# Order of h_lo, conv taps and scan input products in the first half of each tile of a gated-SSM and ternary-FFN kernel

## The reference

```
# block 1
z  = layernorm(x);  u, v = split(z @ in_proj_w + in_proj_b)          # 512 -> 2 x 512
v  = silu(v);       vl = depthwise_conv3(v) + conv_b                   # along time
h_t = a * h_{t-1} + ssm_b * vl_t;   y_t = ssm_c * h_t + ssm_d * vl_t    # scan along time
g  = (u * silu(y)) @ out_proj_w + out_proj_b
x  = x + layernorm(layernorm(g + z) * ln_w + ln_b)
# block 2, weights W1 and W2 rounded to -1, 0, 1 by their mean absolute value
h  = gelu(layernorm(x) @ W1.T + b1)                                    # 512 -> 2048
x  = x + layernorm(h @ W2.T + b2)                                      # 2048 -> 512
```

## Time and profile before

| | us |
|---|---|
| median of 3 runs | 1448.06 (1447.77 to 1449.75) |
| the profiled execution, its own time | 1449.17 |
| its span, first to last instruction | 1447.1 |
| TensorE busy | 1406.8 (97%) |
| VectorE busy | 1118.3 (77%) |
| ScalarE busy | 875.6 (61%) |
| GpSimd busy | 449.6 (31%) |

### The profile page before, as it was taken

The page is one execution under the profiler, slowest core; times in us unless marked ns, Lnnn a source line. Parts: engine busy times, 40 slices in busy tenths (PEclk is TensorE's granted clock), DMA queues, the critical chain, the costliest instruction groups (busy, mean ns, idle before and its releaser), DMA issues. The chain is left out here.

```text
span 1447.1 us, 18964 instructions
## 1 busy us (share of the span) xinstructions
PE 1406.8 (97%) x6492; PEld 635.1 (44%) x6492; DVE 1118.3 (77%) x1891; ACT 875.6 (61%) x1261; POOL 449.6 (31%) x522
## 2 busy tenths in 40 slices
PE   6998999999999999999999999999999999999997
PEld 4443444444444444444444444444444444443443
DVE  8898886877968677786877968678786877998634
ACT  7887665655656566565655656566565655753443
POOL 5146132331523315132321523215142331522211
PEclk9999999999999999999999999999999999999999
DMA  9612221221113112121131113112121221001200
GB/s 264 206 55 80 48 77 29 49 69 30 59 30 88 30 30 80 18 78 30 46 72 29 59 30 88 29 30 80 22 74 30 44 73 30 29 1 30 58 30 30
DMA packets 155984, 82.00 MB, mean 57 GB/s; under 512 B 132720, under 2 KB 132720, under 8 KB 155760
## 3 DMA queue, kind: packets, MB, share of 16 engines
q1 hardware_dynamic: 155888, 80.79, 22.4%
HBM read 31.49 MB, written 16.78 MB: 33 GB/s over the span
## 5 line engine op out<-in xcount | busy, mean ns | idle before, releaser
L562 PE MATMUL f2b<-w,ring 128*128 128x512 fp8e5 x1008 | 382.7, 380 | 2.8 <-DVE w L1004 1.2
L563 PE MATMUL f2b<-w,ring 128*128 128x512 fp8e5 x1008 | 382.3, 379 | 0.0
L534 PE MATMUL f1b<-x3T,w 128*128 128x512 f16 x960 | 365.0, 380 | 6.6 <-DVE w L1004 3.0
L535 PE MATMUL f1b<-x3T,w 128*128 128x512 f16 x960 | 365.0, 380 | 0.0
L1283 ACT ACTIVATE ring<-f1b,par 128x512 f32<-128x512 f32 x256 | 175.0, 683 | 227.3 <-PE f1b L535 226.9
L1623 POOL TENSOR_SCALAR ve<-mv 128x4 f32<-128x4 f32 (+2 forms) x89 | 33.8, 380 | 716.1 <-DVE mv L706 715.8
L714 DVE SCALAR_TENSOR_TENSOR ring<-ring,f_sc 128x512 f16<-128x512 f32 x256 | 209.4, 831 | 41.2 <-ACT ring L1293 41.1
L1293 ACT ACTIVATE ring<-ring,f_sc 128x512 f16<-128x512 f32 x256 | 180.3, 711 | 0.0
L501 PE MATMUL misc<-x1T,win_hi 128*128 128x512 f16 x464 | 176.0, 379 | 2.2 <-DVE yb L807 1.4
L502 PE MATMUL misc<-x1T,win_hi 128*128 128x512 f16 x464 | 176.0, 379 | 0.0
L503 PE MATMUL misc<-x1T,win_lo 128*128 128x512 f16 x464 | 176.0, 379 | 0.0
(11 more groups left out here) (211 smaller groups left out, 2032.2 us busy)
## 6 DMA issues: line engine op xcount, KB each, us to landing
out_dram<-hb SPq DMA_DIRECT2D x64, 256.0 KB, 2.0
xs<-x_dram SPq DMA_DIRECT2D x14, 1024.0 KB, 5.4
ring<-w1t_dram SPq DMA_DIRECT2D x3, 1024.0 KB, 8.0
stage<-w2t_dram SPq DMA_DIRECT2D x3, 1024.0 KB, 8.1
x1T<-tp SPq DMA_TRANSPOSE x68, 3.1
xs<-x_dram SPq DMA_DIRECT2D x4, 256.0 KB, 3.3
stage<-w_in_dram SPq DMA_DIRECT2D x4, 256.0 KB, 5.0
xs<-x_dram SPq DMA_DIRECT2D x2, 512.0 KB, 6.6
```

What stands on the lines that cost most here:

```text
L534: pe.matmul(b[:, :], w, src[:, k, :], start=k == 0, stop=False)
L535: mm = pe.matmul(b[:, :], w, src[:, KC + k, :], start=False, stop=k == KC - 1)
L562: pe.matmul(f2b[q][:, :], h_hi[:, i % H_SLOTS, qs], w2[:, j, :], start=j == 0, stop=False)
L563: mm = pe.matmul(f2b[q][:, :], h_lo[:, i % H_SLOTS, qs], w2[:, j, :], start=False, stop=j == FC - 1)
```

## The change

Three numbers change. In the first half of every stage in which tile c is convolved (stages 2 to 15), VectorE issues lo(3) in front of tap 2 of channel block 2 instead of behind it. ScalarE issues d_conv(c, 2) behind gelu(6) and hi(5), and d_conv(c, 3) behind gelu(7) and hi(6); before, both stood in front of gelu(6). In stage 2 the Sign with the number 5.3 then stands in front of both, and the Sign with 6.5 between them. No instruction, wait or buffer changes.

```diff
-AT_LO = (1.2, 2.2, 2.32, 2.42, 3.36)
-AT_D_CONV, AT_CENTRE = (3.15, 3.16, 5.25, 5.3), (13.3, 13.5, 14.3, 14.5)
+AT_LO = (1.2, 2.2, 2.32, 2.38, 3.36)
+AT_D_CONV, AT_CENTRE = (3.15, 3.16, 6.15, 7.15), (13.3, 13.5, 14.3, 14.5)
```

## The result

Before 1448.13 us, after 1446.12 us (medians of 19 runs each); the ratio of all runs is 0.9983, 95% interval 0.9976 to 0.9989, or -2.5 us (-3.5 to -1.6); the medians alone are 2.0 us apart. The profiled execution took 1446.71 us, its span is 1444.7. The same kernel was measured once more beside the last experiments: 0.9986 (0.9977 to 0.9994), -2.0 us. So the change is a small gain, and it is the difference of two larger numbers.

The account below looks back on a forecast made before the run. TensorE, busy for 97% of the span, was taken to bound the kernel, so only its waits count. Steady stages -5.4 us plus stage 2 +2.6 us gave -2.8 us, 1445.3 us against the median of 1448.06; range 1442.6 to 1449.5 us.

Parts of the forecast that it names:

- The steady term: TensorE's waits at f2(3) and f1(8), mainly in stages 4 to 15, vanish: -5.4 us.
- The margin at f2(4): Steady stages: lo(4) ends 0.6 us before f2(4) wants it, so no new wait there.
- rival C: Steady stages: lo(4) comes late at f2(4), +0.5 us in ten stages, 1455.7 us; chance 0.08.
- Stage 2's rigid shift: Stage 2: later products delay the scans, piece 11 and f1(8), with nothing hiding it: +3.6 us.
- The clock's part: Stage 2: slow stretch falls on f2(3), f1(8) may run at full clock, so the stage costs +2.6 instead of +3.6.
- rival A: Stage 2: slow stretch stays in front of f1(8), full +3.6 us, sum -1.8, 1446.3 us; chance 0.25.
- The sum: Whole kernel: -5.4 us steady plus 2.6 us in stage 2 gives -2.8 us, 1445.3 us; chance 0.50.
- Two bounds of the prediction: Steady stages: lo(4) 1.0 us late gives 4.3 of 5.4 us back; range top 1449.5 us, gain half given back.
- B: Stage 2 costs nothing, as TensorE does not wait for the ternary pieces: -5.4, 1442.7 us; chance 0.08.
- D: Products land between the same neighbours, or gaps come from issuing; only stage 2 tells: 1448 to 1451.7 us; chance 0.09.

Follow-up runs that it names:

- dconv_only: Kernel before with only the ScalarE move: d_conv(2) behind hi(5), d_conv(3) behind hi(6), lo(3) unmoved; 1.0006, +0.9 us against before.
- lo4_late: stage2_old with lo(4) behind scan(2) instead of in front of it, in all stages; 1.0011, +1.6 us against before.
- stage2_only: Kernel before with the new d_conv order on ScalarE in stage 2 alone, lo(3) unmoved; 1.0027, +3.9 us against before.
- stage2_old: Changed kernel with the old d_conv order kept in stage 2, lo(3) swapped there too; 0.9957, -6.2 us, again 0.9964, -5.2 us against before.
- lo_only: Kernel before with only the VectorE swap: lo(3) in front of tap 2 of block 2; 1.0006 against before.
- lo56_early: stage2_old with ternary pieces 11 to 19, lo(5) and lo(6) in front of the scans in stage 2; 0.9953, -6.8 us against before.

## Why the prediction was right

**The steady term: right, slightly small.** Forecast -5.4 us; from stage 3 to the end the two profiles differ by 5.8 us. The transposes' waits at the starts of stages 8 and 14 are different in each execution, here 0.20 and 0.45 us instead of 0.44 and 0.22, by chance the same sum. The missing 0.4 us have two sources: the 20 distances, each less 0.216 us, sum to 5.15 us and not to 5.05, and some 0.02 us per stage lie in the distances right behind the two waits (0.22 to 0.23 us), which were not summed. A stage became 0.54 us shorter, not 0.50. dconv_only, which leaves the first wait, has half of the gain. The margin at f2(4) of 0.6 us, on which rival C hung, is confirmed by lo4_late. C did not come about: GpSimd's additions start 11.9 us into stage 7 and last 6.8 us in both kernels.

**Stage 2's rigid shift: right.** Forecast 3.6 us for piece 11, measured 3.64; less the 0.36 us by which stage 2 begins later, both products start at the forecast times (111.05 and 114.74). The shift went through to the end of the stage: 3.7 us in the table.

**The clock's part: this term failed.** I took +2.6 for stage 2, and so 1.0 us given back, because the slow stretch would lie on f2(3) and spare f1(8). Windows of the changed kernel at f2(3) and at f1(8) in its first profile, then in its second (columns as in the earlier trace rows):

```profile
118.20:121.60 3.40, 2.68 (x8) 0.74 (x6) 3.40 (x6) 0.00 (x0) 0.00 (x0) 0.58 0.00 0
121.90:125.60 3.70, 3.70 (x9) 1.31 (x10) 3.70 (x6) 0.09 (x1) 0.00 (x0) 0.51 0.56 193
```
```profile
122.20:125.40 3.20, 3.20 (x8) 0.88 (x6) 3.20 (x6) 0.00 (x0) 0.00 (x0) 0.50 0.00 0
125.80:129.80 4.00, 3.93 (x15) 1.65 (x16) 4.00 (x8) 1.16 (x2) 0.00 (x0) 0.78 0.66 215
```

In the first, the second half of f2(3) is slow and f1(8) is slow throughout (clock 0.51, near 1.2 GHz): the slow stretch comes twice, nothing returns, and stage 2 costs the full 3.6 us, as rival A had it. In the second, all of f2(3) is slow, and f1(8) for four matmuls only: about 0.9 us return against f1(8) of before. dconv_only's profile is like the first, stage2_only's like the second. But the old order varies too: in the second profile of stage2_old, f1(8) waits 2.01 us as before and is not slow at all:

```profile
120.40:124.10 3.70, 3.60 (x17) 1.68 (x18) 3.70 (x7) 1.67 (x3) 3.70 (x1) 1.00 0.64 197
```

Over all profiles the slow matmuls from f1(8) on cost 1.3 us on average with the new order (four profiles) and 1.4 us with the old one (five), so that nothing is given back on average. The medians agree: stage 2's cost is 3.9 us in stage2_only, 3.8 and 3.2 us between the changed kernel and stage2_old in its two measurements, and 3.8 us in dconv_only (0.9 plus the 2.9 won). None of them alone, with an interval of more than 1 us to either side, excludes 2.6; all lie above it. The Trainium skill ("TensorE: Matmul & The Clock Gate", Part 1) says that the gate's switching is not tied to the kernel's matmuls; the two profiles of one kernel agree: f1(8) is slow for eight matmuls in one and for four in the other, at the same place.

**The sum: close in part by luck.** The gain was put 0.4 us too small and the price about 1.0 us too small, and the two errors offset each other. The profiles make -5.8 + 3.7 = -2.1 us of it; measured are -2.5 (-3.5 to -1.6) and -2.0 us, and forecast (-2.8) and rival A (-1.8) both lie in the interval. The sum doesn't decide between them; the parts are for A's stage 2. Two bounds of the prediction don't come out of their own words: 0.4 us in ten stages gives 4.0 us back and not 4.3, and a steady gain half given back ends at 1448.0 to 1449.0 us and not at 1449.5.

**A comparison of spans alone would have misled.** Stage 2 of the profile of before ends with an accident: its four x3T transposes took 6.41 us to issue, and stage 3 waited 1.78 us for them; after it is 5.53 us and 0.97 us. Without these 0.8 us stage 2's difference of 3.0 us is 3.8, and this agrees with the 3.6 us between dconv_only and lo_only. A slow start of 2.4 us would mislead as much, the other way.

**Rivals B and D** are out: stage2_only costs 3.9 us, and each half of the change moves the wait that it was said to move.

## What to carry to other kernels

Two waits in a row on one engine, with different causes, don't simply add up. Where the second ends at a time that the first has no part in, removing the first alone only lengthens the second (lo_only, 0 us); removing the second alone wins its own part (2.9 us), and the first is worth something only once the second is gone (another 2.9). When a hand-set order is changed for the steady loop, look at the stages where the same numbers sort against other work: here one of 14 stages paid 3.7 us of the 5.8 that the others won, and leaving it in its old order doubled the gain. A term for the clock that rests on one profile is a guess: of five profiles with the old order of stage 2, one shows no slow stretch at f1(8). A matmul is drawn longer than its distance to the next, so short waits of TensorE are read from start to start and not from the idle column.

## What the runs showed of the hardware

- TensorE's slow matmuls (0.43 us apart instead of 0.216) come and go between executions at places where nothing differs: at the start of stage 2 they cost 0 in the profile of before, 2.5 us in that of lo56_early; behind a wait of 2.0 us at f1(8) they cost 1.7 us in four profiles of the old order (granted clock 0.54 in that of before) and nothing in a fifth (clock 1.00). The stretch before stage 2 varies from 91.28 to 95.39 us, partly for the same reason: from 20 to 40 us the granted clock is 0.83 in before (93.45 us) and 1.00 in stage2_old (91.28 us). Medians of 5 to 19 runs average over this; single spans are comparable only in parts.
- A VectorE operation beside GpSimd's 128x512 additions took 1.68 to 1.75 us instead of 0.74, whichever of the two swapped operations stood there: the stretch belongs to the place in time and not to the instruction. A scan took 2.29 instead of 1.27 us there. No run moved the additions, so that they are the cause is a reading and not a test.
